# A graph attention layer: the gathers add node rows onto loaded edge attributes, in place of a VectorE sum

## Chip, cores and metric

One core of a Trainium2 chip runs the whole network as one program. The metric is the device time of one execution in microseconds, as a median of runs. TensorE is called PE in the profile, VectorE DVE, ScalarE ACT, GpSimd POOL and SyncE SP.

## What is computed

A graph network of 12500 nodes with 64 features and 212500 edges, sorted by destination (`dst`). First comes a two-headed attention layer with edge attributes, the "heads layer", then three plain attention layers. Only the heads layer matters here:

```python
h = jnp.maximum(_layernorm(x), 0.0)                      # 12500 x 64
h_edge = ((h[src] + edge_attr) @ W).reshape(-1, H, D)    # 212500 edges, H = 2, D = 64
el = jnp.einsum('ehd,hd->eh', h_edge, attn_l)
er = jnp.einsum('nhd,hd->nh', (h @ W).reshape(-1, H, D), attn_r)
s = leaky_relu(el + er[dst], 0.2)
ex = jnp.exp(s - segment_max(s, dst)[dst])
alpha = ex / segment_sum(ex, dst)[dst]
ft = segment_sum(h_edge * alpha[..., None], dst)         # then the mean over heads
```

## The kernel before

A first stage (`list_units`, L103, with the class `FirstNodes`, L423) makes a list of units and, beside it, the table `h_in`: for each node its 64 normalised features, then two scores for its use as a source and two for its use as a destination, 68 floats or 272 bytes a row. SyncE stores the table in five chunks (`store_chunks`, L412) once the unit lists are made, and waits for all of it (L171). Then comes a barrier of all engines.

The heads layer is `attention_layer` (L592). A unit is a block of 125 destination nodes and up to 2304 edges, which lie as Q = 18 columns of 128. Seventeen columns are always gathered and the last, the tail, only where a unit needs it. There are 100 units here. All tiles that are loaded exist four times (RING = 4). The engines run the same loop over units side by side and meet at semaphores:

- SyncE (`load_unit`) loads for a unit its numbers, the source indices `idx`, the destinations, the edge attributes `edges` (544 KB and 32 KB for the tail) and the block's own rows. The edges of a unit go out when the unit four before it has been weighted (`rows_weighted`).
- GpSimd (`gather`, L832) issues one indirect DMA for each column: 128 rows of `h_in` into `rows_in`. It waits for `rows_taken` (VectorE is through with the rows of the unit four before) and for the indices.
- TensorE turns pairs of edge columns (L1125), multiplies them with the folded score weights (L1135) and so gets the edges' own scores of unit n+1 during unit n. The order of its queue in one unit is: turn the column maxima (L1175), turn the pairs of n+1 (L1125), expand node values to edges (L1184), project the result (L1150), score the pairs of n+1 (L1135), turn the result (L1158), aggregate (L1199), turn the next one-hot (L1142).
- ScalarE copies the edge scores out of PSUM (L1042), then writes 36 masked chunks, 18 for each head (L1087), each from the mask and one column of scores. Later it copies the one-hot (L1093) and the turned pairs (L1033), takes the exponentials (L1104) and makes the next mask (L1048).
- VectorE (`weigh`) adds the gathered source score to the edge score (L949, `scores_sum`) and the gathered rows onto the edges (L951), takes the maximum over columns of the masked chunks in two parts for each head (L962, the first part over 12 chunks), builds the next one-hot (L890), finishes the unit before (L899 to L906), computes the maxima and splits them (L973 to L984), reads the expanded values (L992), forms the logits (L995 to L1000) and weighs the edges for both heads (L1005) with the weights from ScalarE.

The order of work on each engine is written out by hand. `own_steps` (L88) makes VectorE wait for its own last instruction; `wait_apart` (L81) is a wait with an instruction of its own.

Of the kernel before, what the change touches and what calls it, by code (L numbers as in the profile page):

```python
# [23 lines left out]
P = 128  # L24
D = 64
# [397 lines left out]
class FirstNodes:  # L423
# [3 lines left out]
    def __init__(self, nc, con, ctx, x, attn_l, attn_r, w, table, heads):  # L427
# [6 lines left out]
        self.con, self.x, self.attn, self.w, self.table, self.heads = con, x, (attn_l, attn_r), w, table, heads  # L434
# [21 lines left out]
    def store(self, sp):  # L456
        store_chunks(sp, self.table, self.rows_out, self.nb, self.products_copied, self.stored)
        sp.wait_ge(self.stored, 16 * chunks_of(self.nb))
# [133 lines left out]
def attention_layer(nc, con, name, units, src, dst, table, out, edge_attr=None, attn_l=None, w_out=None,  # L592
                    bias=None, residual=None, next_weights=None):
# [12 lines left out]
    first = edge_attr is not None  # L606
    heads = 2 if first else 1
# [3 lines left out]
    out_cols = D if (first or residual is not None) else ROW  # L611
    OUT_LAG = 3 if residual is None else 2
# [4 lines left out]
    with ExitStack() as ctx:  # L617
# [27 lines left out]
        rows_in = ring(sb, "rows_in", [P, Q, row])  # L645
# [29 lines left out]
        if first:  # L675
            edges = ring(sb, "edges", [P, Q, D])
            pairs_t = sb("pairs_t", [P, Q // 2, P])
            edge_scores = sb("edge_scores", [P, Q, heads])
            scores_sum = sb("scores_sum", [P, Q, heads])
            w_cols = sb("w_cols", [P, heads * D])  # L680
            al = sb("al", [P, heads * D])
            wl = sb("wl", [P, heads])
            pair_w = sb("pair_w", [P, 2 * heads])
            w_heads = sb("w_heads", [P, D])
        else:
            bias_sb = sb("bias_sb", [NB, D])
            self_row = sb("self_row", [NB, part])
            self_max = sb("self_max", [NB, 1])
            if residual is not None:
                res_sb = ring(sb, "res_sb", [NB, D])  # L690
            else:
                ext = extend_weights(nc, sb, "ext", *next_weights)
# [37 lines left out]
        with nc.Block() as block:  # L730
            @block.sync
            def _(sp):
# [23 lines left out]
                def load_unit(u, h, k, wait):  # L756
# [13 lines left out]
                    if first:  # L770
                        load_window(edges[h], edge_attr, edge0, edges_loaded[h])
                    sp.dma_start(own[h][:, :], table[bass.ds(node0, NB), :]).then_inc(own_loaded[h], 16)

                def load_residual(n, h):
                    if residual is not None:
                        node0 = node0_of(unit_int[h])
                        if not isinstance(n, int):
                            wait_apart(sp, out_made, n + 2 - RING, passed_sp)
# [959 lines left out]
```

## Time and profile before

| | |
|---|---|
| median of 3 runs | 9685.74 us (9682.82 to 9686.35) |
| the profiled execution's own time | 9684.33 us |
| its span, first to last instruction | 9682.6 us |
| PE busy | 4703.6 us (49%) |
| DVE busy | 7293.6 us (75%) |
| ACT busy | 4571.6 us (47%) |
| POOL busy | 6825.3 us (70%) |
| GpSimd's gathers in the plain layers (L1401) | 5139, 966 ns each |
| ScalarE's masked chunks in the heads layer (L1087) | 3600, 385 ns each |

The shares are of the whole span, in which the plain layers take about seven of ten parts. Busy times of an engine don't say that it bounds: that is read from a timeline, by who waits for whom. A row's bracket gives the idle time of the engine just before the instruction and what ended it; "issue" there is time in which the engine waited for nothing that the profile shows. Rows of one line that follow each other are merged, with their count. Matmuls of 32-bit data show two records each.

### The profile page before, as it was taken

Reading aid. Unit: us, or ns where it says so; the run is one execution under the profiler, and the core shown is the slowest. Engines: PE = TensorE matmul, PEld = TensorE weight load, DVE = VectorE, ACT = ScalarE, POOL = GpSimd, SP = SyncE. Lnnn points to the kernel's source line nnn. Section 1 sums busy time; section 2 is a strip of 40 time slices with the busy share of each in tenths; the row PEclk is TensorE's granted clock in tenths of the full one; section 3 lists DMA queues with packets and bytes.
Section 4 is the critical chain, followed back from the end, with each engine's and each line's share of the span. In section 5 each row is a group of like instructions: output and inputs, shape, how many; then the busy total and the mean of one; then the engine's idle time right before and its main releaser. Section 6 shows DMA issues by size and latency. Waiting matters only on the chain. (4 is left out here: it accounts for less than half of the span.)

```text
span 9682.6 us, 124500 instructions
## 1 busy us (share of the span) xinstructions
PE 4703.6 (49%) x23637; PEld 4345.3 (45%) x23637; DVE 7293.6 (75%) x12031; ACT 4571.6 (47%) x12182; POOL 6825.3 (70%) x6888
## 2 busy tenths in 40 slices
PE   4566666666634444444444444444444444444444
PEld 3565666656634444444443444444443333333333
DVE  2788888888855777777776777777776777777777
ACT  1666666666633444444443444444443444444443
POOL 0777777777713777777776777777776777777776
PEclk9666666666655555555555555555555555555555
DMA  1222222222211111111111111111111111111111
GB/s 43 56 54 51 52 49 52 51 49 52 51 45 42 31 31 31 31 31 31 31 31 27 31 31 31 31 31 31 31 31 27 32 33 32 32 32 32 32 32 30
DMA packets 675572, 360.03 MB, mean 37 GB/s; under 512 B 549773, under 2 KB 550477, under 8 KB 675022
## 3 DMA queue, kind: packets, MB, share of 16 engines
q0 software_dynamic: 220896, 237.06, 13.3%
q1 hardware_dynamic: 454626, 122.45, 6.2%
q14 instruction: 37, 0.30, 0.0%
q8 instruction: 13, 0.21, 0.0%
HBM read 335.55 MB, written 23.35 MB: 37 GB/s over the span
## 5 line engine op out<-in xcount | busy, mean ns | idle before, releaser
L1401 POOL DMA_INDIRECT plain_rows_in<-table,plain_idx x5139 | 4965.7, 966 | 1590.8 <-issue 1590.8
L1649 PE MATMUL plain_ps_sums<-plain_rows_in,plain_prob 128*125 x10908 | 2435.1, 412 | 7.7 <-ACT plain_prob L1612 7.7
L1649 PEld LDWEIGHTS plain_ps_sums<-plain_rows_in,plain_prob 128*125 128x125 f32 x10908 | 2374.4, 329 | 33.4 <-ACT plain_prob L1612 8.3
L832 POOL DMA_INDIRECT heads_rows_in<-h_in,heads_idx x1713 | 1840.4, 1074 | 626.7 <-issue 626.4
L1612 ACT ACTIVATE plain_prob<-plain_prob 128x2250 f32<-128x2250 f32 x300 | 623.6, 2079 | 1845.6 <-DVE plain_prob L1537 1845.6
L1670 PE MATMUL plain_ps_max<-ident,plain_column_max 128*125 128x128 f32 x300 | 173.0, 577 | 2529.1 <-DVE plain_column_max L1518 2529.1
L1670 PEld LDWEIGHTS plain_ps_max<-ident,plain_column_max 128*125 128x125 f32 x300 | 85.2, 284 | 2605.6 <-DVE plain_column_max L1518 2605.6
L1603 ACT ACTIVATE plain_score_sb<-plain_mask,plain_rows_in 128x125 f32<-128x125 f32 x1800 | 553.9, 386 | 1318.6 <-DMA plain_rows_in<-table,plain_idx 1318.6
L1512 DVE TENSOR_TENSOR plain_top<-plain_score_sb,plain_ps_score 128x750 f32<-128x750 f32 x300 | 280.8, 936 | 1149.9 <-ACT plain_ps_score L1603 1149.9
L1087 ACT ACTIVATE heads_masked<-heads_mask,heads_scores_sum 128x125 f32<-128x125 bf16 x3600 | 1053.5, 385 | 62.1 <-DVE heads_scores_sum L949 62.1
L1603 ACT ACTIVATE plain_ps_score<-plain_mask,plain_rows_in 128x125 f32<-128x125 f32 x3600 | 1058.9, 347 | 0.0
L962 DVE TENSOR_REDUCE heads_part_max<-heads_masked 128x125 f32<-128x1500 f32 (+1 forms) x400 | 901.9, 2255 | 187.4 <-ACT heads_masked L1087 163.0
L1463 DVE SCALAR_TENSOR_TENSOR plain_mask<-plain_mask,plain_ps_er 128x2250 f32<-128x2250 f32 x303 | 757.2, 2499 | 150.3 <-PE plain_ps_er L1629 150.1
L1537 DVE TENSOR_TENSOR plain_prob<-plain_prob,plain_ps_max 128x2250 f32<-128x2250 f32 x300 | 749.7, 2499 | 71.2 <-PE plain_ps_max L1674 71.2
L1461 DVE TENSOR_TENSOR plain_mask<-plain_ps_max,plain_dst_local 128x2250 f32<-128x2250 f32 x303 | 758.0, 2502 | 10.4
L1608 ACT ACTIVATE plain_small<-plain_ps_score 128x1500 f32<-128x1500 f32 x300 | 426.2, 1421 | 592.0 <-DVE plain_top L1513 592.0
L1199 PEld LDWEIGHTS heads_ps_acc<-heads_weighted,heads_onehot 128*125 128x125 f32 x3600 | 625.1, 270 | 0.0
L1629 PE MATMUL plain_ps_er<-ident,plain_er_wide 125*128 125x125 f32 x303 | 141.8, 468 | 990.2 <-ACT plain_er_wide L1568 990.2
L1199 PE MATMUL heads_ps_acc<-heads_weighted,heads_onehot 128*125 128x130 f32 x3600 | 621.5, 353 | 0.0
L1629 PEld LDWEIGHTS plain_ps_er<-ident,plain_er_wide 125*128 125x128 f32 x303 | 55.4, 183 | 1046.7 <-issue 577.7
L1524 DVE TENSOR_TENSOR plain_prob<-plain_small,plain_ps_score 128x1500 f32<-128x1500 f32 x300 | 515.4, 1718 | 10.4
L1175 PE MATMUL heads_ps_edge<-ident,heads_column_max 128*125 128x128 f32 x200 | 79.1, 499 | 809.5 <-DVE heads_column_max L964 809.5
(236 smaller groups left out, 7419.3 us busy)
## 6 DMA issues: line engine op xcount, KB each, us to landing
plain_rows_in<-table,plain_idx POOLq DMA_INDIRECT x5139, 2.4
heads_edges<-in_edge_attr SPq DMA_DIRECT2D x104, 544.0 KB
heads_rows_in<-h_in,heads_idx POOLq DMA_INDIRECT x1713, 2.4
plain_own<-table SPq DMA_DIRECT2D x312, 32.7 KB
table<-plain_out_sb SPq DMA_DIRECT2D x200, 32.7 KB
n_x<-in_x SPq DMA_DIRECT2D x2, 3125.0 KB
plain_unit_int<-unit_ints SPq DMA_DIRECT2D x312, 0.0 KB
plain_idx<-in_src SPq DMA_DIRECT2D x312, 8.5 KB
```

Of the source, the lines that this page charges most:

```text
L832: gp.indirect_dma_start(rows_in[h][:, t, :], None, table[:, :], bass.IndirectOffsetOnAxis(ap=idx[h][:, t:t + 1], axis=0)).then_inc(done, 16)
L962: step(ve.tensor_reduce(part_max[k][:, hd, :], masked[:, hd, cols, :] .rearrange("p t n -> p n t"), AX.X, ALU.max))
L1087: ins = ac.activation(masked[:, hd, t, :], mask[:, t, :], ACT.Identity, bias=score)
L1199: ins = te.matmul(ps_acc[0:NB, 0:heads * part], onehot[h][:, t, :], weighted[:, t, :], start=t == 0, stop=t == Q - 1)
L1401: gp.indirect_dma_start(rows_in[h][:, t, :], None, table[:, :], bass.IndirectOffsetOnAxis(ap=idx[h][:, t:t + 1], axis=0)).then_inc(done, 16)
L1461: step(ve.tensor_tensor(tile, bcast(iota, 1, Q), bcast(dst_local[:, :], 2, NB), ALU.not_equal))
L1463: ve.scalar_tensor_tensor(tile, tile, -BIG, bcast(er_row, 1, Q), ALU.mult, ALU.add).then_inc(mask_made, 1)
L1524: ve.tensor_tensor(tile[:, THIRD:Q, :], small[:, :, :], score_ps, ALU.max).then_inc(scores_taken, 1)
L1537: ve.tensor_tensor(tile[:, :, :], tile[:, :, :], bcast(max_row, 1, Q), ALU.subtract).then_inc(logits_made, 1)
L1603: ins = ac.activation(score_sb[:, t, :] if t < THIRD else score_ps[:, t - THIRD, :], mask[h % 2][:, t, :], ACT.Identity, bias=rows_in[h][: ...
L1612: ac.activation(prob[h % 2][:, :, :], prob[h % 2][:, :, :], ACT.Exp).then_inc(weights_made, 1)
L1649: ins = te.matmul(sums[h % 2], prob[h % 2][:, t, :], rows, start=t == 0, stop=t == Q - 1)
```

## The change

The heads layer gets a function of its own, `heads_layer`; what it drops from `attention_layer` for other layers was not in use there. In it:

- The first stage writes the 64 normalised features of each node a second time, to `x_rows` with rows of 256 bytes, ahead of the table on the same queue.
- SyncE loads the edge attributes into `rows`. GpSimd waits for them (`edges_loaded`), and its gathers read `x_rows` and add onto `rows` in the DMA (`compute_op=ALU.add`). There is no `rows_in`, no `rows_taken` and no clearing of its tail.
- TensorE turns the pairs of the sums and not of the edges, so it waits for the gathers (`gathered`, `tail_ready`) where it waited for the edges. The score that it gets is the whole score of the edge.
- VectorE drops `scores_sum` (L949) and the sum of rows (L951). ScalarE makes the masked chunks from `edge_scores` and waits for its own copy of them. VectorE's wait for the gathers moves down to the weighing.
- Since unit n+1 is turned during unit n, the gathers run one unit further than the last.

The core of the diff:

```diff
@@ FirstNodes
     def store(self, sp):
+        store_chunks(sp, self.rows, self.rows_out[:, :, 0:D], self.nb, self.products_copied, self.stored)
         store_chunks(sp, self.table, self.rows_out, self.nb, self.products_copied, self.stored)
-        sp.wait_ge(self.stored, 16 * chunks_of(self.nb))
+        sp.wait_ge(self.stored, 32 * chunks_of(self.nb))
...
@@ SyncE
-                    if first:
-                        load_window(edges[h], edge_attr, edge0, edges_loaded[h])
+                    load_window(rows[h], edge_attr, edge0, edges_loaded[h])
...
@@ GpSimd
-                    gp.indirect_dma_start(rows_in[h][:, t, :], None, table[:, :],
-                                          bass.IndirectOffsetOnAxis(ap=idx[h][:, t:t + 1], axis=0)
-                                          ).then_inc(done, 16)
-                for h in range(RING):
-                    gp.memset(rows_in[h][:, Q - 1, :], 0.0).then_inc(tails_set, 1)
-                gp.wait_ge(tails_set, RING)
+                    gp.indirect_dma_start(rows[h][:, t, :], None, x_rows[:, :],
+                                          bass.IndirectOffsetOnAxis(ap=idx[h][:, t:t + 1], axis=0),
+                                          compute_op=ALU.add).then_inc(done, 16)
...
-                        gp.wait_ge(rows_taken[h], i + 1)
+                        gp.wait_ge(edges_loaded[h], 32 * i + 32)
...
+                wait_apart(gp, edges_loaded[0], 32 * rounds + 32, passed_gp)
+                wait_apart(gp, idx_loaded[0], 32 * rounds + 32, passed_gp)
+                for t in range(Q - 1):
+                    gather(0, t, gathered[0])
+                gp.sem_inc(tail_ready[0], 1)
...
@@ VectorE
                 def weigh(i, h, n, k_next, step):
-                    ve.wait_ge(gathered[h], 16 * (Q - 1) * i + 16 * (Q - 1))
-                    ve.wait_ge(tail_ready[h], i + 1)
                     ve.wait_ge(own_loaded[h], 16 * i + 16)
-                    if first:
-                        ve.wait_ge(scores_copied, n + 1)
-                        ve.wait_ge(edges_loaded[h], 32 * i + 32)
-                        ve.tensor_tensor(scores_sum[:, :, :], edge_scores[:, :, :], rows_in[h][:, :, D:D + heads],
-                                         ALU.add).then_inc(scores_ready, 1)
-                        ve.tensor_tensor(edges[h][:, :, :], edges[h][:, :, :], rows_in[h][:, :, 0:D], ALU.add
-                                         ).then_inc(rows_taken[h], 1)
...
+                    ve.wait_ge(scores_copied, n + 1)
...
                     ve.wait_ge(weights_made, 2 * n + 3)
-                    rows = edges[h] if first else rows_in[h]
+                    ve.wait_ge(gathered[h], 16 * (Q - 1) * i + 16 * (Q - 1))
+                    ve.wait_ge(tail_ready[h], i + 1)
...
@@ ScalarE
-                        if first:
-                            ac.wait_ge(scores_ready, n + 1)
+                        ac.wait_ge(scores_copied, n + 1)
...
@@ TensorE
                 def turn_pairs(n, k, h):
 
-                    te.wait_ge(edges_loaded[h], 32 * k + 32)
+                    te.wait_ge(gathered[h], 16 * (Q - 1) * k + 16 * (Q - 1))
+                    te.wait_ge(tail_ready[h], k + 1)
```

## Rows read from the trace of the kernel before

**Rows 1.** The page, part 5, gathers of the layer: count | busy, mean ns | idle.

```profile
L832 POOL DMA_INDIRECT heads_rows_in<-h_in,heads_idx x1713 | 1840.4, 1074 | 626.7 <-issue 626.4
```

**Rows 2.** Timeline, VectorE, one unit: start, us, engine, line, what [idle before, releaser].

```profile
1498.97 2.66 DVE L1005 TENSOR_TENSOR heads_weighted<-heads_edges,heads_weights 128x1152 f32<-128x1152 f32 x2 [0.30 <-ACT heads_weights L1104]
...
1501.97 0.20 DVE L949 TENSOR_TENSOR heads_scores_sum<-heads_edge_scores,heads_rows_in 128x36 f32<-128x36 f32 x1 [0.24 <-ACT heads_edge_scores L1042]
1502.09 1.35 DVE L951 TENSOR_TENSOR heads_edges<-heads_edges,heads_rows_in 128x1152 f32<-128x1152 f32 x1
...
1505.88 4.66 DVE L962 TENSOR_REDUCE heads_part_max<-heads_masked 128x125 f32<-128x1500 f32 x2 [1.63 <-ACT heads_masked L1087]
...
1518.74 0.17 DVE L902 TENSOR_SCALAR heads_inverse<-heads_acc 125x2 f32<-125x2 f32 x1
...
1523.87 2.63 DVE L1005 TENSOR_TENSOR heads_weighted<-heads_edges,heads_weights 128x1152 f32<-128x1152 f32 x2 [0.30 <-ACT heads_weights L1104]
```

**Rows 3.** Timeline, ScalarE, the same stretch.

```profile
1501.55 0.20 ACT L1042 ACTIVATE heads_edge_scores<-heads_ps_out 128x36 f32<-128x36 f32 x1
1502.26 10.54 ACT L1087 ACTIVATE heads_masked<-heads_mask,heads_scores_sum 128x125 f32<-128x125 bf16 x36 [0.52 <-DVE heads_scores_sum L949]
...
1526.59 0.20 ACT L1042 ACTIVATE heads_edge_scores<-heads_ps_out 128x36 f32<-128x36 f32 x1
```

**Rows 4.** Timeline, TensorE, the same stretch.

```profile
1518.84 2.13 PE L1125 MATMUL heads_ps_big<-ident,heads_edges 128*128 128x128 f32 x9
1521.53 0.65 PE L1184 MATMUL heads_ps_edge<-heads_node_split,heads_onehot_t 125*128 125x12 bf16 x18 [0.56 <-DVE heads_node_split L984]
...
1522.48 3.95 PE L1135 MATMUL heads_ps_out<-heads_pair_w,heads_pairs_t 128*128 128x4 f32 x18
```

**Rows 5.** Timeline, GpSimd, the same stretch.

```profile
1502.74 1.51 POOL L832 DMA_INDIRECT heads_rows_in<-h_in,heads_idx  x1 [0.31 <-issue]
1504.56 0.94 POOL L832 DMA_INDIRECT heads_rows_in<-h_in,heads_idx  x1 [0.30 <-issue]
...
1512.06 2.10 POOL L832 DMA_INDIRECT heads_rows_in<-h_in,heads_idx  x1 [0.30 <-issue]
```

**Rows 6.** Groups by line, GpSimd, 264.4 to 874.1 us, then 1477 to 2482 us.

```profile
L832 POOL DMA_INDIRECT heads_rows_in<-h_in,heads_idx x451 | 473.9, 1051 | 137.4 <-issue 137.1 <-DMA heads_idx<-in_src 0.3
...
L832 POOL DMA_INDIRECT heads_rows_in<-h_in,heads_idx x683 | 742.8, 1087 | 262.0 <-issue 262.0
```

**Rows 7.** Timeline, VectorE, two units early in the layer.

```profile
306.61 0.41 DVE L902 TENSOR_SCALAR heads_inverse<-heads_acc 125x2 f32<-125x2 f32 x1
...
312.32 2.66 DVE L1005 TENSOR_TENSOR heads_weighted<-heads_edges,heads_weights 128x1152 f32<-128x1152 f32 x2 [0.30 <-ACT heads_weights L1104]
...
337.65 2.66 DVE L1005 TENSOR_TENSOR heads_weighted<-heads_edges,heads_weights 128x1152 f32<-128x1152 f32 x2 [0.30 <-ACT heads_weights L1104]
```

**Rows 8.** Timeline, SyncE's DMA issues, from the first stage on.

```profile
198.21 6.63 SPq L419 DMA_DIRECT2D h_in<-n_rows  x5
228.41 0.48 SPq L793 DMA_DIRECT2D heads_w_cols<-in_L_gnn_W  x1
...
237.38 0.33 SPq L747 DMA_DIRECT2D heads_edges<-in_edge_attr  x1
```

**Rows 9.** DMA queues, 200 to 226 us: packets, MB, share of 16 engines.

```profile
q1 hardware_dynamic: 631, 3.30, 31.5%
```

**Rows 10.** DMA queues, 1534.0 to 1534.5 us, a store to h_heads.

```profile
q1 hardware_dynamic: 119, 0.03, 26.0%
```

**Rows 11.** Timelines, first unit of the layer: VectorE, TensorE, ScalarE.

```profile
264.32 0.20 DVE L949 TENSOR_TENSOR heads_scores_sum<-heads_edge_scores,heads_rows_in 128x36 f32<-128x36 f32 x1 [21.81 <-DMA heads_rows_in<-h_in,heads_idx]
...
241.91 2.15 PE L1125 MATMUL heads_ps_big<-ident,heads_edges 128*128 128x128 f32 x9 [46.81 <-DMA heads_edges<-in_edge_attr]
...
249.45 0.20 ACT L1042 ACTIVATE heads_edge_scores<-heads_ps_out 128x36 f32<-128x36 f32 x1 [4.09 <-PE heads_ps_out L1135]
```

**Rows 12.** Timeline, GpSimd, the first stage's only gather.

```profile
18.93 3.90 POOL L220 DMA_INDIRECT edge_row<-in_dst,row_of_i  x1 [7.17 <-DVE row_of_i L240]
```

## What the change should do to the time

> **What bounds the kernel now.** I read the page's list of costly groups first, to see which stage the change touches, then the timelines of one unit in the middle of the heads layer, engine by engine, and last the queues. The change touches the heads layer (100 units of up to 2304 edges) and the last store ahead of it. The three plain layers behind it share nothing with the change and are taken as unchanged.
>
> One unit lasts 24.90 us mid-layer, from one L1005 to the next [rows 2], and 25.33 us early in the layer [rows 7]; I take 25.1 as its mean. VectorE is nearly full, but the ring that closes it is wider than VectorE. Follow it: the column maxima (L962) start at 1505.88 and run on without a gap to the node split, which releases TensorE at 1521.53 [rows 2, 4]; TensorE expands, projects and scores the next unit's edge pairs until 1522.48 + 3.95 = 1526.43 [rows 4]; ScalarE copies those scores at 1526.59 [rows 3]; in the next unit VectorE adds the gathered score (L949), ScalarE makes twelve masked chunks from it, and L962 starts again. The vector sum L951 (1.35 us) that the change removes is not on this ring: right behind it VectorE stands idle 1.63 us until ScalarE's masked chunks are there [rows 2]. Whoever takes 100 x 1.35 us as the gain reads a busy time as a path.
>
> GpSimd is the second engine to watch. It issued 1713 gathers for 100 units, 17.13 a unit [rows 1]. While it ran unhindered, 451 of them took 473.9 + 137.4 = 611.3 us [rows 6], 1.355 us each, so 23.2 us a unit. It gains on VectorE by some 2 us a unit until its ring of four is full. It is within a tenth of being the bound.
>
> **The change part by part.** *The hop is removed.* The masked chunks now wait for ScalarE's own score copy and not for L949. Before, the copy started at 1501.55 and took 0.20; the chunks started at 1502.26 [rows 3], 0.51 us behind its end. A hand-over to itself is in no row here; it lies between nothing and 0.24 us, VectorE's idle time behind the copy [rows 2]. I take 0.10, so the ring shortens by 0.41 us (0.27 to 0.51), 41 us in 100 units.
>
> *L951 and L949 go.* On VectorE that is 1.35 + 0.20 us under the wait for ScalarE: nothing, since that wait only grows. If the cover were gone it would be worth 1.5 us a unit. GpSimd gains, though: the gather that began at 1502.74, under L951, took 1.51 us and the next 0.94 [rows 5], so 0.57 us a unit comes off GpSimd: 23.2 - 0.57 = 22.6 us a unit. The gather at 1512.06, under the one-hot build, still pays (2.10 us) [rows 5]. The Trainium skill (SBUF — State Buffer, Who interferes with whom) says that a VectorE instruction with two SBUF inputs contends with a GpSimd instruction that reads SBUF; the slow gathers agree.
>
> *The gather adds.* Its rows shrink from 272 to 256 bytes, which is worth nothing in issue. What the addition costs GpSimd is in no row. The nearest is the same gather without it, 0.94 us [rows 5]; a far one is the only other indirect load, 3.90 us for 101 long rows [rows 12]. I take 0.94, because destination, index form and row count stay; below it there is no reason for a gain. The ends stay for the range. The price matters from a definite point: a unit of 22.6 us against one of 25.1 - 0.41 = 24.7 leaves 2.1 us, so 2.1 / 17.13 = 0.12 us a gather. Below that it is hidden; above it every further 0.1 us costs 171 us.
>
> *New waits.* GpSimd waits for the edge rows of a unit before gathering it; behind that stand only later gathers. SyncE loads them once the unit four before has been weighted, and the first load landed 241.91 - 237.38 = 4.5 us after its issue [rows 8, 11]. TensorE now waits for the gather before turning pairs, and behind that wait in its queue stands the expansion of the unit in hand. The turn sits 5.0 us ahead of the weighting of its own round (1518.84 against 1523.87) [rows 2, 4], so from one load to the turn that needs it there are about three units less 8 us, 66 us; load and gathers need 4.5 + 22.6 + some 2. Nothing, while GpSimd keeps pace. Without that cover the unit costs what GpSimd costs.
>
> *The start.* The first gathers wait for the edges: at best from 241.91. Before, they went 2.4 us earlier, beside the scoring, which was over at 249.65, and the first unit began at 264.32 [rows 11]. Now turning, copying and scoring (249.65 - 241.91 = 7.7 us) come behind the gathers: 2.4 + 7.7 = 10 us, once. A unit more of gathers at the end is hidden as long as GpSimd is ahead.
>
> *The second store.* The normalised rows are written once more, 12500 x 256 B = 3.2 MB, ahead of the table on SyncE's queue. The stores are issued only when the unit lists are made, at 198.21, and the heads layer starts when they have landed, at 228.41 [rows 8], so the new one lies on the path with nothing beside it. The table's store uses 31.5% of 16 engines, five of them, at 3.30 MB in 26 us [rows 9]. At that rate 3.2 MB take 25 us. But the new one is read in pieces of 256 bytes, and pieces of that size took 0.260 x 16 x 0.5 us / 119 = 17.5 ns of an engine each [rows 10]: 12500 x 17.5 / 5 = 44 us. I take 45, since the piece decides; 25 stays as the low end.
>
> **Sum.** -41 + 10 + 45 = +14 us on a span of 9682.6. The profiled execution's own time was 9684.3 and the median of the runs 9685.7, so the forecast is 9685.7 + 14 = 9700. With the ends of the terms (-51 and 25, -27 and 50, the start 8 to 20) the likeliest case has 9665 to 9730.
>
> **The rivals.** *GpSimd becomes the bound, a quarter dearer.* An adding gather has to name what it reads in the tile too. At 0.94 + 0.24 = 1.18 us a unit takes 22.6 + 17.13 x 0.24 = 26.7 us. The last turn then waits for the gathers of the hundredth further unit, at 266.7 + 2670 = 2937, where before it came near 264.3 + 99 x 25.1 + 16.9 = 2766; so +171, and +45: 9900. For it speaks that only 0.12 us is free; against it, that nothing in the row count grows.
>
> *GpSimd bound, half as dear again.* If reading the destination as well makes each row half as dear again to issue, 0.94 becomes 1.41: 22.6 + 8.1 = 30.7 us a unit, last turn at 3337, +571 + 45: 10300. The Trainium skill (DMA: Bandwidth & Descriptors) gives one read and one write descriptor for each plain operation (SWDGE vs HWDGE vs iDMA) and says of an accumulating DMA that it reads its destination and writes it later (Rules for kernel authors); it names no price, and no row of before shows an accumulating gather.
>
> *The slow form.* At 3.90 us a gather [rows 12] a unit takes 17.13 x (3.90 + 0.30) + 1.3 = 73 us: near 14500.
>
> *The other side: collisions go.* Short VectorE instructions on the ring are held up while GpSimd issues: L902 took 0.41 us early and 0.17 mid-layer [rows 2, 7], and the unit 25.33 against 24.90. If GpSimd, done sooner and then waiting for edges, is out of the way there, all units run at 24.90 - 0.41 = 24.5: -61. With the store at the byte rate, 25 us, the sum is -61 + 10 + 25 = -26: 9660. It ends on the faster side only from 0.74 us a unit at 45 us for the store (74 - 55 = 19), or 0.54 at 25. Against it: the store's small pieces.
>
> *The change doesn't do what it says*: it then leaves the hop in place, because the copy waits for something else; that is the low end of the first term, +28 to +50, inside the range.
>
> **How the numbers follow.** About 0.2%, 19 us, is what a measurement of this kernel can tell from no change. Forecast case 0.42; a quarter dearer 0.23; half dearer 0.15; slow form 0.08; collisions gone 0.12. The range goes from 9655, the faster rival nearly whole, to 10300, the half-dearer one; left out are the slow form and the outer parts of those two, about 0.2. Slower: 0.46 of the three GpSimd cases and two fifths of the forecast case (above 9705), 0.61. Faster: three quarters of the last rival and a little of the forecast, 0.12. The rest, 0.27, is within 0.2%.
>
> **What would show it.** Right: L1087 starts about 0.1 us behind L1042; VectorE's idle time before L962 grows to near 3 us; the heads layer starts 45 us later; gathers stay at 0.94 us with one idle stretch a unit in GpSimd. Wrong: gathers above 1.06 us, no idle stretch in GpSimd, TensorE's L1125 waiting for a gather and VectorE's L992 behind it. A store that adds 25 us, or well above 50, would make the second term wrong, and a unit under 24.5 us the first.

## The result, and the profile after

The changed kernel takes 10557.2 us (median of 4 runs, 10556.8 to 10558.3) beside 9685.3 for the kernel before on the same chip: a ratio of 1.0901, with a 95% interval of 1.0882 to 1.0920. The forecast was 9700 and its range ended at 10300. The runs below went to several chips, and each is compared with the kernel before on its own chip (9685 to 9703 us). On one chip the kernel before took 12841 us. Four kernels ran there: e8 (11986.4 us), the eleven columns (e10, 11248.7), the hop alone (e11, 12612.6) and the order alone (e12, 12843.8). The times of this chip are compared with no others: e11 and e12 have units of 37.9 and 37.6 us there, e10 one of 24.59, and why is open. e13 to e15 are the last three on a chip of the usual time.

The page of the changed kernel: its span, part 1 (busy us of each engine), and from part 5 the gathers (L802) and the reduction that opens the second half of a unit's VectorE work (L916, which was L992).

```profile
span 10555.1 us, 124243 instructions
...
PE 4734.5 (45%) x23637; PEld 4363.9 (41%) x23637; DVE 7103.6 (67%) x11831; ACT 4571.3 (43%) x12182; POOL 7825.8 (74%) x6901
...
L802 POOL DMA_INDIRECT heads_rows<-x_rows,heads_idx x1730 | 2840.7, 1642 | 782.8 <-issue 782.8
...
L916 DVE TENSOR_REDUCE heads_edge_vals<-heads_ps_edge 128x72 f32<-128x216 f32 x100 | 38.3, 383 | 866.3 <-PE heads_ps_edge L1085 866.3
```

A gather costs GpSimd 1642 ns in the mean where it was 1074 [rows 1], so its busy time in this layer goes from 1840 to 2841 us. VectorE's share falls to 67%: it waits 866 us before L916.

What one line did, first the gathers and then the weighing in the kernel before, then the weighing in the changed kernel. The columns are ns as minimum/median/maximum, and the first and last start in us.

```profile
L832 POOL DMA_INDIRECT heads_rows_in<-h_in,heads_idx x1713: 938/944/3285, 239.6 to 2693.9; - x191
...
L1005 DVE TENSOR_TENSOR heads_weighted<-heads_edges,heads_weights x200: 1344/1356/1394, 286.7 to 2781.8; 128x1152 f32<-128x1152 f32 x100
```

```profile
L929 DVE TENSOR_TENSOR heads_weighted<-heads_rows,heads_weights x200: 1344/1356/1419, 349.4 to 3654.8; 128x1152 f32<-128x1152 f32 x100
```

There are 100 units of two weighing instructions, the second 1.3 us behind the first. Before, a unit lasts (2781.8 - 1.3 - 286.7) / 99 = 25.19 us; after, (3654.8 - 1.3 - 349.4) / 99 = 33.37 us. The first weighing is 62.7 us later. So the loss is 62.7 + 99 x 8.18 = 873 us, against 872 measured. This way of splitting a difference is used for every run below.

The timeline of the changed kernel, one unit in mid-layer, all engines (start, us, engine, line, what, [idle before, releaser]).

```profile
1503.08 1.54 POOL L802 DMA_INDIRECT heads_rows<-x_rows,heads_idx  x1 [0.30 <-issue]
...
1504.93 1.54 POOL L802 DMA_INDIRECT heads_rows<-x_rows,heads_idx  x1 [0.30 <-issue]
...
1509.31 0.16 DVE L907 TENSOR_TENSOR heads_node_split<-heads_rest,heads_node_split 125x4 bf16<-125x4 f32 x1
...
1515.57 2.17 PE L1032 MATMUL heads_ps_big<-ident,heads_rows 128*128 128x128 f32 x9 [8.51 <-DMA heads_rows<-x_rows,heads_idx]
...
1517.55 0.67 PE L1085 MATMUL heads_ps_edge<-heads_node_split,heads_onehot_t 125*128 125x12 bf16 x18
...
1518.31 0.38 DVE L916 TENSOR_REDUCE heads_edge_vals<-heads_ps_edge 128x72 f32<-128x216 f32 x1 [8.56 <-PE heads_ps_edge L1085]
...
1519.90 2.63 DVE L929 TENSOR_TENSOR heads_weighted<-heads_rows,heads_weights 128x1152 f32<-128x1152 f32 x2 [0.30 <-ACT heads_weights L1012]
...
1521.53 2.40 POOL L802 DMA_INDIRECT heads_rows<-x_rows,heads_idx  x1 [0.30 <-issue]
...
1523.25 0.20 ACT L962 ACTIVATE heads_edge_scores<-heads_ps_out 128x36 f32<-128x36 f32 x1
...
1523.64 10.53 ACT L998 ACTIVATE heads_masked<-heads_mask,heads_edge_scores 128x125 f32<-128x125 bf16 x36 [0.20 <-ACT heads_edge_scores L962]
...
1527.26 4.68 DVE L887 TENSOR_REDUCE heads_part_max<-heads_masked 128x125 f32<-128x1500 f32 x2 [3.86 <-ACT heads_masked L998]
```

Beside the old unit [rows 2 to 5] it reads: VectorE has its node split ready at 1509.47, and TensorE could turn it into edge values, but ahead of that expansion (L1085) in TensorE's queue stands the turn of the next unit's pairs (L1032), which waits 8.51 us for that unit's gathers. VectorE waits 8.56 us behind it. GpSimd never waits: every start follows the last end by 0.30 us. One unit of it is 17.13 gathers of 1.54 + 0.30 us, 31.5, and the two that meet VectorE's weighing (L929) and its one-hot build (L855), 2.40 us at 1521.53 and 2.62 at 1533.46, add 1.9, which makes 33.4.

The stores at the end of the first stage, SyncE's timeline of the changed kernel.

```profile
198.26 28.07 SPq L419 DMA_DIRECT2D x_rows<-n_rows  x5
226.37 10.47 SPq L419 DMA_DIRECT2D h_in<-n_rows  x5
263.52 0.48 SPq L771 DMA_DIRECT2D heads_w_cols<-in_L_gnn_W  x1
```

The next stage begins at 263.52 where it began at 228.41 [rows 8]: 35.1 us for the second store.

The software queue of GpSimd between 1500 and 2000 us, the kernel before and then the changed one (packets, MB, share of 16 engines).

```profile
q0 software_dynamic: 10816, 11.79, 12.6%
```

```profile
q0 software_dynamic: 37003, 8.44, 19.5%
```

The first window holds 339 gathers and the second 257: 32 packets a gather before, 144 after, which is one for each of 128 rows and 16 more. In the same window e4 (64 rows) has 22079 packets for 276 gathers and e8 (32 rows) 13610 for 283, so 80 and 48: again one a row and 16 more.

### The profile page after: what moved, and what is told of

Same layout as the page of the kernel before. It is cut to its first block and busy times, and to the rows that moved or that the text cites. A ratio compares the mean times of both kernels' runs of the same rounds, so it can differ in the third digit from the quotient of the medians.

```text
span 10555.1 us, 124243 instructions
## 1 busy us (share of the span) xinstructions
PE 4734.5 (45%) x23637; PEld 4363.9 (41%) x23637; DVE 7103.6 (67%) x11831; ACT 4571.3 (43%) x12182; POOL 7825.8 (74%) x6901
## 5 line engine op out<-in xcount | busy, mean ns | idle before, releaser
L802 POOL DMA_INDIRECT heads_rows<-x_rows,heads_idx x1730 | 2840.7, 1642 | 782.8 <-issue 782.8
L1545 PEld LDWEIGHTS plain_ps_sums<-plain_rows_in,plain_prob 128*125 128x125 f32 x10908 | 2375.0, 330 | 32.9 <-ACT plain_prob L1508 8.3
L998 ACT ACTIVATE heads_masked<-heads_mask,heads_edge_scores 128x125 f32<-128x125 bf16 x3600 | 1053.3, 384 | 11.7 <-ACT heads_edge_scores L962 4.7
L953 ACT ACTIVATE heads_pairs_t<-heads_ps_big 128x512 f32<-128x512 f32 (+1 forms) x303 | 126.8, 491 | 1508.9 <-PE heads_ps_big L1032 1508.9
L1032 PE MATMUL heads_ps_big<-ident,heads_rows 128*128 128x128 f32 x909 | 218.7, 424 | 979.6 <-DMA heads_rows<-x_rows,heads_idx 549.2
L916 DVE TENSOR_REDUCE heads_edge_vals<-heads_ps_edge 128x72 f32<-128x216 f32 x100 | 38.3, 383 | 866.3 <-PE heads_ps_edge L1085 866.3
L1032 PEld LDWEIGHTS heads_ps_big<-ident,heads_rows 128*128 128x128 f32 x909 | 179.9, 223 | 1007.5 <-issue 1007.5
```

The lines of the kernel that those rows point to most:

```text
L802: gp.indirect_dma_start(rows[h][:, t, :], None, x_rows[:, :], bass.IndirectOffsetOnAxis(ap=idx[h][:, t:t + 1], axis=0), compute_op=ALU.add ...
L998: ins = ac.activation(masked[:, hd, t, :], mask[:, t, :], ACT.Identity, bias=edge_scores[:, t, hd:hd + 1])
L1545: ins = te.matmul(sums[h % 2], prob[h % 2][:, t, :], rows, start=t == 0, stop=t == Q - 1)
```

## The experiments

Theory A: the price of issuing an adding gather, multiplied by 17.13 a unit, is the whole loss, and GpSimd is the bound. Rival B: the new waits (TensorE for the gathers, GpSimd for the edges) make a longer ring, whatever a gather costs. Rival C: the small writes of the addition hold up the data, and the store and the start matter more than thought.

**e1, without the addition.** The changed kernel with all its waits, its two stores and its order, but the gathers overwrite the edge attributes in place of adding to them, so these are missing from the sums.

```diff
-                                          bass.IndirectOffsetOnAxis(ap=idx[h][:, t:t + 1], axis=0),
-                                          compute_op=ALU.add).then_inc(done, 16)
+                                          bass.IndirectOffsetOnAxis(ap=idx[h][:, t:t + 1], axis=0)
+                                          ).then_inc(done, 16)
```

> The changed kernel with plain gathers: they overwrite the loaded edge attributes instead of adding onto them, so the edge attributes are left out of the sum; every wait, load, store and order is that of the changed kernel. Theory A (the adding gather is dearer to issue on GpSimd, 1.54 us against 0.94, and GpSimd sets the unit): the gather falls back to 0.94 us, a unit to about 24.7 us, the time to 9685 + 35 (the second store as the trace of after shows it) + 10 (start) - 41 (hop) = 9690, between 9665 and 9720. Theory B (the new waits make load, gather and turning one chain behind each other, whatever a gather costs): the time stays above 10200.

Measured: 9728.8 us beside 9702.9, 1.0027 (1.0016 to 1.0038), +26 us. The gathers and the weighing of e1, in the view by line:

```profile
L802 POOL DMA_INDIRECT heads_rows<-x_rows,heads_idx x1730: 938/944/3285, 279.1 to 2765.5; - x193
...
L929 DVE TENSOR_TENSOR heads_weighted<-heads_rows,heads_weights x200: 1344/1356/1396, 335.7 to 2809.3; 128x1152 f32<-128x1152 f32 x100
```

One unit of e1, VectorE and ScalarE:

```profile
1504.21 0.41 DVE L867 TENSOR_SCALAR heads_inverse<-heads_acc 125x2 f32<-125x2 f32 x1
...
1506.80 0.31 DVE L906 CAST heads_node_split<-heads_rest 125x4 bf16<-125x4 f32 x1
...
1512.42 0.20 ACT L962 ACTIVATE heads_edge_scores<-heads_ps_out 128x36 f32<-128x36 f32 x1
...
1512.82 10.53 ACT L998 ACTIVATE heads_masked<-heads_mask,heads_edge_scores 128x125 f32<-128x125 bf16 x36 [0.20 <-ACT heads_edge_scores L962]
...
1516.43 4.67 DVE L887 TENSOR_REDUCE heads_part_max<-heads_masked 128x125 f32<-128x1500 f32 x2 [2.99 <-ACT heads_masked L998]
```

The gathers are back at 944 ns and the loss of 9% is gone. Rival B falls, since all its waits are in this kernel. The masked chunks start 0.20 us behind the end of the score copy (1512.62 to 1512.82) where it was 0.51 [rows 3], and VectorE's wait before the column maxima is 2.99 us, so the hop is gone as predicted. But a unit lasts 24.97 us, only 0.22 less, where 24.7 was expected: short VectorE instructions met by a gather give part back (L867 took 0.41 us, L906 0.31). In the mean of all units the chunks start 0.12 us behind the copy where it was 0.50, and the stretch from the start of the column maxima to the end of the node split is 15.90 us where it was 15.73. The first gains 0.38, the second gives back 0.17. L867 alone has a mean of 0.40 us, against 0.27 for L902 before.

**e2, the addition alone.** The kernel before with the one flag; its tiles are cleared once and then never, so its sums run on from unit to unit and are not the reference's. Nothing else moves.

```diff
-                                          bass.IndirectOffsetOnAxis(ap=idx[h][:, t:t + 1], axis=0)
-                                          ).then_inc(done, 16)
+                                          bass.IndirectOffsetOnAxis(ap=idx[h][:, t:t + 1], axis=0),
+                                          compute_op=ALU.add).then_inc(done, 16)
...
-                    gp.memset(rows_in[h][:, Q - 1, :], 0.0).then_inc(tails_set, 1)
+                    gp.memset(rows_in[h][:, :, :], 0.0).then_inc(tails_set, 1)
```

> The kernel before with the one flag: its gathers of h_in rows add onto rows_in (cleared once at the start) instead of overwriting it, so the rows hold running sums over units and the output is not the layer's. No wait is moved, the sums on VectorE stay. Theory A: a gather takes 1.54 us, GpSimd has 17.13 x 1.84 + 1.8 + 0.6 = 34 us of work a unit, the layer grows by 100 x (34 - 25.1) = 890 us less a little: 10450 to 10600. Theory B: the time stays within 100 us of 9685, since the waits are those of before and the gathers run ahead by three units.

Measured: 10573.6 us beside 9702.9, 1.0898 (1.0876 to 1.0920), +871 us, the whole loss of the change.

```profile
L832 POOL DMA_INDIRECT heads_rows_in<-h_in,heads_idx x1713: 1531/1540/3492, 239.3 to 3625.8; - x191
...
L1005 DVE TENSOR_TENSOR heads_weighted<-heads_edges,heads_weights x200: 1344/1356/1421, 295.4 to 3651.9; 128x1152 f32<-128x1152 f32 x100
```

A gather takes 1540 ns and a unit (3651.9 - 1.3 - 295.4) / 99 = 33.89 us. The flag alone is enough. That its total meets the changed kernel's so closely is partly chance: its unit is 0.52 us dearer than the changed kernel's, and its first weighing comes 54 us sooner.

**e6, the second store alone**, on the kernel before.

```diff
+        store_chunks(sp, self.rows, self.rows_out[:, :, 0:D], self.nb, self.products_copied, self.stored)
         store_chunks(sp, self.table, self.rows_out, self.nb, self.products_copied, self.stored)
-        sp.wait_ge(self.stored, 16 * chunks_of(self.nb))
+        sp.wait_ge(self.stored, 32 * chunks_of(self.nb))
```

> The kernel before with the second store alone: the normalised rows are also written to x_rows ahead of the table, and nothing reads them. Both theories: the heads layer starts 35 us later, as in the changed kernel, and the time is 9685 + 35 = 9720. My forecast had 45 from the packet price, with 25 from the byte rate as the low end; a value of 25 to 30 would say that part of the 35 us comes from elsewhere.

Measured: 9736.6 us beside 9702.9, 1.0035 (1.0023 to 1.0048), +34 us. The heads layer begins at 263.69, 35.3 us later than in the kernel before [rows 8]:

```profile
263.69 0.48 SPq L795 DMA_DIRECT2D heads_w_cols<-in_L_gnn_W  x1
```

**e3, half the row length.** The changed kernel adds 32 of the 64 features, in rows of 128 bytes; the other half of the sums lacks the node rows. `x_rows` and its store are half as wide as well.

```diff
-                    gp.indirect_dma_start(rows[h][:, t, :], None, x_rows[:, :],
+                    gp.indirect_dma_start(rows[h][:, t, 0:D // 2], None, x_rows[:, :],
```

> The changed kernel with rows half as long: the gathers add 32 of 64 features (128 bytes of each of 128 rows), x_rows holds 32 columns; the other half of the node rows is left out of the sum. Theory A1 (the price of adding is GpSimd's work for each row, whatever its length): a gather stays at 1.54 us and the time near 10550, less some 15 us for the smaller store. Theory A2 (the price is data: the DMA engines add slowly and GpSimd is held up by full queues): a gather falls to about 1.24 us.

```profile
L802 POOL DMA_INDIRECT heads_rows<-x_rows,heads_idx x1730: 1532/1541/3352, 272.9 to 3636.5; - x193
```

10573.7 us beside 9699.9 (one run of each), and 1541 ns a gather: the bytes don't matter. The price is not that of the data that is read and added. The smaller store brought the first weighing 6 us forward (343.4 for 349.4), not the 15 expected.

**e4 and e5, half the number of rows**, with the addition and without. Only 64 partitions get node rows.

```diff
-                    gp.indirect_dma_start(rows[h][:, t, :], None, x_rows[:, :],
-                                          bass.IndirectOffsetOnAxis(ap=idx[h][:, t:t + 1], axis=0),
+                    gp.indirect_dma_start(rows[h][0:P // 2, t, :], None, x_rows[:, :],
+                                          bass.IndirectOffsetOnAxis(ap=idx[h][0:P // 2, t:t + 1], axis=0),
```

> The changed kernel with gathers of 64 rows instead of 128, all 64 features, adding; the edges on partitions 64 to 127 get no node row. Theory A1 (work for each row plus a fixed part): adding costs more a row than plain; if all of the extra 0.60 us is per row, this gather takes 0.30 us more than the plain one of 64 rows (next run), and if it is a fixed extra, 0.60 us more. GpSimd's unit shrinks to 17.13 x (about 1.0 + 0.3) + 1.8 = 24 us and the time to about 9700.

> As the run before, without the adding: 64 rows, plain, overwriting the edges of those partitions. A gather takes between 0.47 us (all by row) and 0.94 us (all fixed); I expect 0.65. The time is near 9690, since GpSimd has slack.

The gathers of e4, then those of e5:

```profile
L802 POOL DMA_INDIRECT heads_rows<-x_rows,heads_idx x1730: 1403/1412/3244, 279.3 to 3441.6; - x193
```

```profile
L802 POOL DMA_INDIRECT heads_rows<-x_rows,heads_idx x1730: 903/912/3223, 279.6 to 2741.5; - x193
```

e4 took 10376.0 us and e5 9711.7, beside 9699.9 (one run of each). Both expectations were misses, as most of the price was taken to go by the row: e4's gather was put near 1.0 us and its time near 9700, e5's gather at 0.65 us. Adding costs 1412 - 912 = 500 ns with 64 rows and 1540 - 944 = 596 ns with 128. A straight line through these two has 1.5 ns a row and 404 ns that would be there with no row at all.

**e8, a quarter of the rows**, which tells a fixed part from one that only flattens out. Only 32 partitions get node rows. It ran on the chip of 12841 us, so its total is not read, only its gathers and its unit, which GpSimd sets alone.

```diff
+                    gp.indirect_dma_start(rows[h][0:32, t, :], None, x_rows[:, :],
+                                          bass.IndirectOffsetOnAxis(ap=idx[h][0:32, t:t + 1], axis=0),
```

> The changed kernel with adding gathers of 32 rows instead of 128; the edges on the other 96 partitions get no node row. 128 rows took 1.54 us and 64 rows 1.41 us, against 0.94 and 0.91 plain. Theory F (the price of adding is mostly a fixed part of each instruction, near 0.4 us, with 2 ns a row on top): 1.41 - 32 x 0.002 = 1.35 us and GpSimd still sets the unit, 17.13 x 1.65 + 1.85 = 30.1 us, the time near 10240. Theory R (by row): it goes on falling towards 1.1 us and the time to near 9800.

```profile
L802 POOL DMA_INDIRECT heads_rows<-x_rows,heads_idx x1730: 1337/1342/3494, 279.2 to 3323.8; - x193
```

1342 ns with 32 rows, 1412 with 64, 1540 with 128: 2.0 to 2.2 ns a row over some 1.27 us that belong to the instruction. GpSimd never waits here either, and a unit lasts 30.17 us, as theory F had it (30.1). The number of packets isn't the price either: carried on to the 32 packets of a plain gather, this line has 1.31 us where that one takes 0.94. The Trainium skill (DMA: Bandwidth & Descriptors, Anatomy of one DMA — SWDGE (gpsimd) path) says that one can emit many descriptors before their own cost shows; here the trace agrees, with 2 ns a row. But the addition raises what is there before any row.

**e13, eleven of seventeen columns.** If GpSimd's total is the whole cause, fewer adding gathers should hide again, dear as each is. Six columns of a unit get no node rows.

```diff
-                        for t in range(Q - 1):
+                        for t in range(11):
...
-                    te.wait_ge(gathered[h], 16 * (Q - 1) * k + 16 * (Q - 1))
+                    te.wait_ge(gathered[h], 16 * 11 * k + 16 * 11)
```

> The eleven-column kernel once more, beside a kernel before of the usual time: adding gathers for 11 of 17 columns, the edges of the other 6 get no node row. In the run before this one the chip was another, on which the kernel before took 12841 us with waits at every hand-over, and no ratio from it says anything of the ring. Theory A (the dear gather costs the kernel only what GpSimd has above the ring): 11.13 x 1.84 + 1.85 = 22.3 us of GpSimd a unit is hidden, ratio 1.001 to 1.005 as with plain gathers. Rival (adding also costs in landing, in the DMA engines or at VectorE's port): above 1.01.

Measured: 9688.7 us beside 9701.6, 0.9986 (0.9977 to 0.9996), -13 us. The gathers, then VectorE over one unit:

```profile
L802 POOL DMA_INDIRECT heads_rows<-x_rows,heads_idx x1124: 1532/1541/3850, 279.7 to 2725.2; - x188
```

```profile
1497.61 4.66 DVE L887 TENSOR_REDUCE heads_part_max<-heads_masked 128x125 f32<-128x1500 f32 x2 [3.23 <-ACT heads_masked L998]
...
1510.40 0.21 DVE L867 TENSOR_SCALAR heads_inverse<-heads_acc 125x2 f32<-125x2 f32 x1
...
1512.74 0.17 DVE L906 CAST heads_node_split<-heads_rest 125x4 bf16<-125x4 f32 x1
...
1522.21 4.66 DVE L887 TENSOR_REDUCE heads_part_max<-heads_masked 128x125 f32<-128x1500 f32 x2 [3.14 <-ACT heads_masked L998]
```

The gather is as dear as in the changed kernel, but 11.13 of 1.84 us are 20.5 us a unit, or 23.2 with the gathers that VectorE holds up (1.78 us in the mean and 0.30 to the next), and they are hidden. All waits of the change and both stores are here too, so A stands and B and C fall. The ratio even lies below the expected 1.001 to 1.005. A unit is 24.60 us, which nearly reaches the 24.5 that the rival of gone collisions gave: L867 takes 0.21 and L906 0.17 us, and the stretch from the column maxima to the node split is 15.51 us in the mean, against 15.73 before and 15.90 in e1.

**e14, the hop alone.** The kernel before, but TensorE adds the gathered score in PSUM, so that VectorE's sum of scores is not on the ring; L951 stays, and gathers don't add. Since TensorE now needs the rows of unit n+1 during unit n, the gathers run one unit further here and in e9.

```diff
+                    te.matmul(ps_out[:, SCORE_AT:SCORE_AT + Q * heads].rearrange("p (t k) -> p t k", k=heads),
+                              con.ident[:, :], rows_in[h][:, :, D:D + heads], start=True, stop=False)
...
-                            ac.wait_ge(scores_ready, n + 1)
+                            ac.wait_ge(scores_copied, n + 1)
```

> The hop-only kernel once more, beside a kernel before of the usual time: L949 replaced by one matmul ahead of the scoring, ScalarE waits for its own copy, order as before. The hop is worth 0.31 us a unit, the matmul costs some 0.35 us on the same ring: ratio 0.998 to 1.002.

Measured: 9712.4 us beside 9701.6, 1.0011 (1.0002 to 1.0021). TensorE and ScalarE over one unit:

```profile
1508.90 0.59 PE L1137 MATMUL heads_ps_out<-heads_rows_in,ident 128*128 128x36 f32 x2
...
1509.30 3.98 PE L1145 MATMUL heads_ps_out<-heads_pair_w,heads_pairs_t 128*128 128x4 f32 x18
...
1513.52 0.19 ACT L1045 ACTIVATE heads_edge_scores<-heads_ps_out 128x36 f32<-128x36 f32 x1
...
1513.80 10.53 ACT L1090 ACTIVATE heads_masked<-heads_mask,heads_edge_scores 128x125 f32<-128x125 bf16 x36
```

The chunks start 0.09 us behind the copy, 0.42 sooner (0.38 in the mean of all units), but the added matmul puts the scoring 0.40 us back on the same ring (1508.90 to 1509.30). One pays for the other.

**e15, the order alone.** The kernel before, with the next unit's turn, the projection and five of nine scoring pairs ahead of the wait for the node split, where TensorE stands idle, and ScalarE's mask sooner.

```diff
+                        if first:
+                            te.wait_ge(onehot_copied, n + 1)
+                            turn_pairs(n + 1, i + (h == RING - 1), after(h))
...
+                            project(n)
+                            score_pairs(n + 1, 0, 5)
...
+                            score_pairs(n + 1, 5, Q // 2)
```

> The order-only kernel once more, beside a kernel before of the usual time: pairs turned, result projected and five pairs scored ahead of the split, mask made earlier, L949 kept on VectorE behind the weighing. The scores are ready early but L949 still starts when the weighing ends: ratio 0.997 to 0.999. Near 0.985 would say that the order alone carried the gain of the fastest version.

Measured: 9674.2 us beside 9701.6, 0.9971 (0.9961 to 0.9982). ScalarE and VectorE over one unit:

```profile
1510.14 0.19 ACT L1042 ACTIVATE heads_edge_scores<-heads_ps_out 128x36 f32<-128x36 f32 x1
...
1512.74 0.18 DVE L949 TENSOR_TENSOR heads_scores_sum<-heads_edge_scores,heads_rows_in 128x36 f32<-128x36 f32 x1
...
1513.02 10.54 ACT L1087 ACTIVATE heads_masked<-heads_mask,heads_scores_sum 128x125 f32<-128x125 bf16 x36 [2.69 <-DVE heads_scores_sum L949]
```

The scores are copied at 1510.33 but the chunks start at 1513.02, behind L949, which stands in VectorE's queue behind the weighing. The ring now closes through that instruction.

**e9, both together**, on the kernel before, without adding gathers. Nothing of the computation is left out.

```diff
+                            turn_pairs(n + 1, i + (h == RING - 1), after(h))
...
+                            project(n)
+                            score_nodes(n + 1, i + (h == RING - 1), after(h))
+                            score_pairs(n + 1, 0, 5)
...
-                            ac.wait_ge(scores_ready, n + 1)
+                            ac.wait_ge(scores_copied, n + 1)
```

> A version from the kernel before with plain gathers and no second store. TensorE adds the gathered score columns to the edge scores in PSUM (one matmul of the identity with 36 columns), so L949 goes and the masked chunks wait for ScalarE's own copy; TensorE turns the pairs and projects ahead of the split it waits for, and scores five of nine pairs there; ScalarE makes the next mask before the turned pairs. VectorE keeps the sum of rows. If the ring VectorE - TensorE - ScalarE - VectorE is what closes a unit, it shortens by some 2.4 us and VectorE or GpSimd's 23.2 us close it: 9685 - 100 x 1.9 = 9495, between 9450 and 9560. If VectorE alone bounds the unit, only its 0.2 us of L949 are gained: 9665.

Measured: 9526.2 us beside 9702.9, 0.9819 (0.9803 to 0.9836), -177 us: faster than both kernels. Its gathers, then one unit of VectorE and ScalarE:

```profile
L831 POOL DMA_INDIRECT heads_rows_in<-h_in,heads_idx x1730: 940/944/2787, 239.7 to 2590.3; - x193
```

```profile
1504.12 2.66 DVE L1008 TENSOR_TENSOR heads_weighted<-heads_edges,heads_weights 128x1152 f32<-128x1152 f32 x2 [0.30 <-ACT heads_weights L1109]
...
1504.56 10.54 ACT L1090 ACTIVATE heads_masked<-heads_mask,heads_edge_scores 128x125 f32<-128x125 bf16 x36
...
1508.57 0.38 DVE L889 TENSOR_SCALAR heads_dst_local<-heads_dst_ids,heads_unit_par 128x18 f32<-128x18 int32 x1
...
1508.72 4.65 DVE L965 TENSOR_REDUCE heads_part_max<-heads_masked 128x125 f32<-128x1500 f32 x2
...
1527.22 2.66 DVE L1008 TENSOR_TENSOR heads_weighted<-heads_edges,heads_weights 128x1152 f32<-128x1152 f32 x2 [0.30 <-ACT heads_weights L1109]
```

The chunks start at 1504.56, beside the weighing, and VectorE goes from L889 into the column maxima (L965) without a wait. A unit is 23.10 us here and 23.35 in the mean. By the page, 1730 gathers took 1824.6 us and the gaps ahead of them 537.7, so 17.13 gathers make 23.4 us a unit. GpSimd is full: no gather starts later than the usual 0.30 us behind the last. VectorE nearly is: beside the 0.30 us before the weighing it waits 0.86 us a unit, for the expanded values (L995). The time lies where the ring was expected to bring it, between 9450 and 9560, and not at the 9665 of a kernel that VectorE alone bounds. e14 (+11 us) and e15 (-27 us) don't add up to this; each leaves the ring closed at the place that the other opens.

Put side by side, all by the two numbers of the weighing's line. "Sum" is the change of the first weighing plus 99 times the change of a unit; it meets the measured difference within 10 us.

```
kernel                       first weighing  us a unit   sum    measured
before                       286.7           25.19
after                        349.4           33.37      +873    +872
e2, addition alone           295.4           33.89      +870    +871
e3, half the row             343.4           33.35      +864    +874
e4, 64 rows, adding          344.9           31.36      +669    +676
e1, no addition              335.7           24.97       +28     +26
e6, second store             321.5           25.21       +37     +34
e5, 64 rows, no addition     335.4           24.75        +5     +12
e13, eleven columns          335.2           24.59       -11     -13
e14, hop alone               292.6           25.24       +10     +11
e15, order alone             286.3           24.91       -28     -27
e9, hop and order            292.4           23.35      -176    -177
```

## Why the prediction was wrong

- **The bound and the margin: right.** The ring, the cover of L951 and GpSimd as the next bound were read rightly, and so was the point from which it decides, 0.12 us a gather with 171 us for every further 0.1: in e1 a unit of 24.97 us holds 22.9 us of GpSimd (1.030 + 0.305 us, 17.13 times), which leaves 0.12 a gather. The price rose by 0.60: (0.60 - 0.12) x 1713 = 822 us from that step alone.
- **The step that failed: "I take 0.94, because destination, index form and row count stay"**. A gather that adds took 1.54 us. What stays is not what sets the price. Of the 0.60 us some 0.2 go by the row (2 ns for 0.5) and 0.4 are there before any row, so they belong to the instruction's kind, which was what changed. The packets show that the transfers are cut another way too, 144 a gather for 32.
- **The rivals.** The mechanism that came true was named with all its signs: gathers above 1.06 us, no idle stretch in GpSimd, TensorE's turn waiting for a gather and VectorE's reduction behind it. Its version next below the measured price had 1.41 us and 10300. With 1.54 the same formula gives 22.6 + 17.13 x 0.60 = 32.9 us a unit and, with 35 for the store, 10512; the last 45 us are the unit's 33.37 for 32.9, since gathers held up by VectorE grow with their length (2.40 and 2.62 us). Its reason, each row half as dear again, was wrong: with a quarter of the rows the gather still takes 1.34 us (e4, e8). So that 1.41 lies near 1.54 is luck, not a mechanism foreseen.
- **The range** stopped at that rival. Between 1.41 and the 3.90 of the far row nothing was priced, though a tenth of a microsecond was worth 171 us there. The far row was also called the only other indirect load, while the plain layers have 5139 at 966 ns each. With bounds of 0.94 and 3.90 on an engine with 0.12 to spare, the forecast rested on the near end of an interval in which nearly every other value loses.
- **The hop: right in size.** 0.41 (0.27 to 0.51) predicted; 0.38 in the mean of all units in e1 and e13, from the start of the chunks behind the copy. That a unit gained only 0.22 in e1 is the collisions' doing: the VectorE stretch of the ring grew by 0.17.
- **The rival of gone collisions: right in size, in a kernel that isn't this one, but not in its reason.** e13 has units of 24.59 us. GpSimd isn't out of the way there, with 23.2 us of work a unit; the traces show another phase. In e13 L867 starts between two gathers in all 101 units, in e1 it starts 0.52 to 0.54 us into a gather in 98 of 101. In the changed kernel the VectorE stretch is as short as in e13 (15.50 us), with GpSimd never idle, and gains nothing, as GpSimd sets the pace.
- **The second store: the term was mis-sized by 10 us.** 45 predicted (25 to 50), 35 measured in the trace and 34 in e6. The 17.5 ns for a piece of 256 bytes came from a store of one unit's result; in the large store it is 35.1 x 5 / 12500 = 14.0 ns, still not the byte rate.
- **The start: 10 predicted (8 to 20), 14 measured** in e1 (335.7 - 286.7 - 35.1). In the changed kernel the first weighing comes another 13.7 us later; 17 gathers that each cost 0.60 more are 10.2 of them.
- **The other waits: right.** With gathers at 0.94 (e1) GpSimd's wait for the edges and TensorE's for the gathers cost nothing in the middle of the layer: TensorE's turn waits for a gather once, at the start.
- **Two slips in the sums, without weight.** With the hop left in place the first term is 0, so that case is 10 + 45 = +55 and not +28 to +50. And 0.46 with two fifths of 0.42 make a chance of 0.63 for slower, not 0.61.

The forecast was +14 us; e1, which is the change without the dear gather, is at +26: the start cost 4 more and the hop gained 20 less than forecast, and the store cost 10 less.

## What to carry to other kernels

Count a DMA that computes as another instruction, not as the same one with a flag: here it cost the issuing engine 0.60 us more for each of 1713 gathers, to save VectorE 1.55 us a unit that lay under a wait. Before work moves to an engine, write down its slack in us per instruction; where that is small beside what an unmeasured form could cost, measure one such instruction first. And two edits that give little or nothing alone (-27 and +11 us) can give much together (-177) when each opens one of two places where the same ring closes.

## What the runs showed of the hardware

- An adding indirect gather costs GpSimd 1540, 1412 and 1342 ns with 128, 64 and 32 rows; a plain one 944 and 912 ns with 128 and 64. Halving the row length (256 to 128 bytes) changed nothing in the adding one (1541 ns). Lines drawn through these points leave 1.27 us before any row in an adding gather and 0.88 in a plain one. Why the addition costs 0.4 us there is open: no run looked inside the instruction.
- It lands 3.0 us after its issue where the plain one took 2.4, and the software queue's engines go from 12.6% to 19.5% busy at three quarters of the gathers in the same time. They were never near full.
- A short VectorE instruction is held at one phase of a plain gather. Two units of the kernel before, gather and L902:

```profile
1543.36 0.94 POOL L832 DMA_INDIRECT heads_rows_in<-h_in,heads_idx  x1 [0.30 <-issue]
...
1543.78 0.17 DVE L902 TENSOR_SCALAR heads_inverse<-heads_acc 125x2 f32<-125x2 f32 x1
...
1593.54 0.94 POOL L832 DMA_INDIRECT heads_rows_in<-h_in,heads_idx  x1 [0.30 <-issue]
...
1594.08 0.40 DVE L902 TENSOR_SCALAR heads_inverse<-heads_acc 125x2 f32<-125x2 f32 x1
```

Of 80 units between 400 and 2400 us, 35 have L902 begin under 0.5 us into a gather, and all take 0.17 us; 25 have it begin 0.51 to 0.54 us in, and all take 0.40 to 0.42, ending as the gather does. Beyond that it is 0.17 to 0.38. The reciprocal right behind it (L903) takes 0.17 us in every unit. In some kernels the phase is nearly the same in every unit: in e1 the counterpart L867 starts 0.52 to 0.54 us into a gather in 98 of 101 cases and takes 0.40 us in the mean; in e5, where a gather is 0.03 us shorter, it starts 0.65 to 0.67 us in, also in 98 of 101, and takes 0.21 to 0.23; in e13 it always starts between two gathers and takes 0.21. So a gain on the ring can be given back by a shift of a few tenths, which moves these instructions into the held stretch. The Trainium skill (SBUF — State Buffer, Who interferes with whom) calls the pair of ports that the two engines share an exclusive lock; the trace agrees that one waits whole, and adds that it does so in a part of the gather alone, about its second half.
- Rows of 256 bytes were stored at 3.2 MB / 35.1 us = 91 GB/s, the table's 3.30 MB at 127 [rows 9].
